# First attention of a fused decoder: heads in pairs, rotation over two banks at once, squared norms streamed

## What is computed

```python
q, k, v = (cproj(Wq), cproj(Wk), cproj(Wv))      # x @ W, real and imaginary halves, (b, n, 16, 64)
qr, kr = q * phase, k * phase                    # phase = cos(ang) + i sin(ang)
s = einsum('bihd,bjhd->bhij', qr, conj(kr)).real
qn = (q.real**2 + q.imag**2).sum(-1)             # kn likewise
E = exp(clip(-mu * |t_i - t_j|, -30, 0))
maha = maximum(qn_i + E*E*kn_j - 2*E*s, 0) / V
logits = coef * log1p(maha / nu) - 0.5*64*log(V), causal
A = softmax(logits); out = A @ v; y = concat(out.real, out.imag) @ Wo
x = layernorm(x + y)
```

## Time and profile before

| | us |
|---|---|
| median of three runs | 3004.72 |
| the runs | 2991.95, 3010.06, 3004.72 |
| span of the profiled execution | 3006.1 |
| TensorE busy in it | 2483.3 (83%) |
| VectorE busy in it | 1809.2 (60%) |

### The profile page before, as it was taken

One profiled execution on the slowest core, in us unless ns is written; L12 is line 12 of the kernel. 1 busy time (PEld: TensorE's weight loads), 2 busy tenths in 40 slices (PEclk: granted clock), 3 DMA queues, 4 the chain that ended last, 5 costly groups with the idle time before them and its releaser, 6 DMA issues.

```text
span 3006.1 us, 41680 instructions
## 1 busy us (share of the span) xinstructions
PE 2483.3 (83%) x14384; PEld 1904.4 (63%) x14384; DVE 1809.2 (60%) x4049; ACT 1131.3 (38%) x2706; POOL 873.9 (29%) x765
## 2 busy tenths in 40 slices
PE   3978979697987979788896979879797888969688
PEld 2666757566675757667575666757576675756544
DVE  8964469524975359634786259653596348852554
ACT  2443325333452325433353324523253333433233
POOL 1531235202541135302452025411353024520100
PEclk8888969797887978889787978879698887879799
DMA  4000000000000000000000000000000000010000
GB/s 152 1 1 1 1 22 1 1 1 22 1 1 1 1 23 1 1 1 1 22 1 1 1 23 1 1 1 1 22 1 1 1 8 15 1 63 1 8 14 14
DMA packets 17083, 32.64 MB, mean 11 GB/s; under 512 B 2686, under 2 KB 8710, under 8 KB 16086
## 3 DMA queue, kind: packets, MB, share of 16 engines
q1 hardware_dynamic: 15574, 25.53, 2.5%
q0 software_dynamic: 1280, 4.20, 0.4%
HBM read 23.43 MB, written 5.77 MB: 10 GB/s over the span
## 4 chain that ended last, share of the span: by engine, by line
PE 54%; DVE 29%; issue 9%; ACT 6%; POOL 1%; DVEq 0%; ACTq 0%; SPq 0%; DMA 0%; POOLq 0%
PE bank L841 50%; DVE work L374 6%; PE bank L845 4%; ACT work L630 4%; DVE work L392 4%; DVE work L383 3%; DVE work L372 2%; DVE st L325 2%; DVE act_row L332 1%; ACT act_T L630 1%; DVE negmax L394 1%; DVE mv L328 1%; ACT ln_t L630 1%; DVE work L528 1%; DVE negmax L525 1%
## 5 line engine op out<-in xcount | busy, mean ns | idle before, releaser
L630 ACT ACTIVATE work<-work 128x512 f32<-128x512 f32 (+1 forms) x584 | 352.2, 624 | 524.1 <-DVE work L528 155.3
L841 PEld LDWEIGHTS bank<-work 128*128 128x128 f32 x3104 | 402.5, 198 | 124.4 <-issue 115.6
L841 PE MATMUL bank<-work 128*128 128x128 f32 x3104 | 429.2, 284 | 40.4 <-DMA work<-in_wo 34.8
L630 ACT ACTIVATE work<-bank 128x512 f32<-128x512 f32 x440 | 250.2, 588 | 312.1 <-PE bank L841 237.3
L374 DVE TENSOR_TENSOR work<-bank,table_space 64x512 f32<-64x512 f32 x512 | 352.3, 688 | 6.8
L823 POOL TENSOR_TENSOR work<-work,sb_cols 128x512 f32<-128x512 f32 x128 | 132.3, 1039 | 742.1 <-ACT work L630 615.9
L841 PE MATMUL bank<-sb_cols,work 128*128 128x1 f32 x2048 | 277.7, 265 | 71.8 <-ACT work L630 71.8
L841 PEld LDWEIGHTS bank<-sb_cols,work 128*128 128x128 f32 x2048 | 275.3, 216 | 91.6 <-ACT work L630 91.6
L630 ACT ACTIVATE work<-bank,sb_b_up 128x512 f32<-128x512 f32 x288 | 197.9, 687 | 270.1 <-PE bank L841 264.8
L841 PEld LDWEIGHTS bank<-sb_w_down,work 128*128 128x128 f32 x2304 | 267.3, 192 | 30.6 <-issue 30.6
L512 DVE SCALAR_TENSOR_TENSOR work<-bank,wexp,work 128x128 f32<-128x128 f32 x256 | 72.1, 344 | 353.9 <-PE bank L841 353.9
(11 more groups left out here) (224 smaller groups left out, 3729.7 us busy)
## 6 DMA issues: line engine op xcount, KB each, us to landing
sb_w_up<-in_w_up SPq DMA_DIRECT2D x1, 2304.0 KB
sb_w_down<-in_w_down SPq DMA_DIRECT2D x1, 2304.0 KB
x_T<-in_x_T POOLq DMA_DIRECT2D x8, 256.0 KB, 2.9
x_row<-in_x_row POOLq DMA_DIRECT2D x8, 256.0 KB, 3.0
ctx_T<-in_ctx_T SPq DMA_DIRECT2D x8, 256.0 KB, 2.9
work<-in_ctx_row SPq DMA_DIRECT2D x8, 256.0 KB, 3.6
out<-act_row SPq DMA_DIRECT2D x8, 256.0 KB, 2.3
x_scratch<-act_row SPq DMA_DIRECT2D x7, 256.0 KB, 2.5
```

The lines of the kernel that those rows point to most:

```text
L630: return nc.scalar.activation(o, i, f, **k)
L841: return nc.tensor.matmul(o, l, r, start=start, stop=stop, skip_group_check=True)
```

## The change

Heads are taken by twos. Step `s` now makes the q (even `s`) or the k (odd `s`) of the pair `p = s // 2`: real parts of both heads in one bank, imaginary parts in the next, the two banks being one tensor `pair_bank` of 128x1024. VectorE multiplies all of it by cosine in one instruction, and by a signed sine with the banks crossed in a second one. GpSimd adds 128x1024 at once. ScalarE squares straight out of `pair_bank`. The norms of a pair are made by a 128x32 selector as the stationary side and the squares as the moving side (`norm_rows_of`, 8 products on 256 columns, each into its own 32 partitions), copied, and turned by two transposes (`norm_cols_of`). The scores of a pair (`scores_of(p)`, steps `s = 2p + 3`) are 16 products of 64 rows instead of 8 of 128, alternating between the row halves of the two heads, into banks 4 and 5. Exponential and scaling work in place in four tiles `M0`. The angle, cosine and sine tables are half as long (8 pairs in place of 16 heads). Pipeline distances grow: distance (`maha`) at step h + 4, logits at h + 5, exponential at h + 6, values and transposes at h + 7, and there are 24 steps in place of 23.

The diff, cut to its added lines and their context (the lines that they replace stand in the functions above; "..." marks what is left out):

```diff
+        pair_bank = ctx.enter_context(nc.psum_tensor("pair_bank", [128, 2, W], fp32))
+        bank = ([pair_bank[:, 0], pair_bank[:, 1]]
+                + [ctx.enter_context(nc.psum_tensor(f"bank{i}", [128, W], fp32)) for i in range(2, 8)])
...
+        table_space = sb("table_space", 128, 4 * H0 * N + 3 * HP * N)
+        dec, dec_inv, wgt, bias_t = (
+            table_space[:, i * H0 * N:(i + 1) * H0 * N].rearrange("p (h n) -> p h n", h=H0) for i in range(4))
+        at = 4 * H0 * N
+        cosT = table_space[:, at:at + HP * N].rearrange("p (h n) -> p h n", h=HP)
+        sin2 = table_space[:, at + HP * N:at + 3 * HP * N].rearrange("p (s h n) -> p s h n", s=2, h=HP)
...
+        by_cos, by_sin = two(0), two(2)
+        q_rot, k_rot = [two(4), two(6)], [two(8), two(10)]
+        sq = [two(12), two(14)]
+        M0 = [wk[16 + i] for i in range(4)]
+        diag = [wk[20], wk[21]]
+        norm_row = wk[22][:, 0:2 * N]
+        attn_space = sb("attn_space", 128, 5, W)
+        v_head = [attn_space[:, i] for i in range(3)]
+        prob_head = [attn_space[:, 3 + i] for i in range(2)]
...
+            for h in range(HP):
                 last = v.tensor_scalar(ang[:, h], tramp[:]
...
+                for s in range(H0 + 8):
+                    if s < H0:
+                        p = s // 2
+                        dve.wait_ge(proj, g * H0 + s + 1)
+                        if s > 0:
+                            dve.wait_ge(rot, g * H0 + s)
+                        R_I = pair_bank[:].rearrange("p r (b n) -> p (r b) n", b=GB)
+                        v.tensor_tensor(by_cos.rearrange("p r (b n) -> p (r b) n", b=GB), R_I,
+                                        cosT[:, p].unsqueeze(1).broadcast_to([128, 2 * GB, N]), ALU.mult)
+                        v.tensor_tensor(by_sin.rearrange("p r (b n) -> p r b n", b=GB),
+                                        pair_bank[:, ::-1].rearrange("p r (b n) -> p r b n", b=GB),
+                                        sin2[:, :, p].unsqueeze(2).broadcast_to([128, 2, GB, N]),
+                                        ALU.mult).then_inc(parts, 1)
+                    h = s - 6
                     if 0 <= h < H0:
                         dve.wait_ge(exped, g * H0 + h + 1)
                         if h >= 2:
                             dve.wait_ge(prob, g * H0 + h - 1)
                         v.reciprocal(rsum[:, h % 2, :], esum[:, h % 4, :]).then_inc(sums_inv, 1)
+                    h = s - 4
                     if 0 <= h < H0:
+                        p, c = h // 2, h % 2
+                        M = rows(M0[h % 4])
+                        dve.wait_ge(norms_sb, g * HP + p + 1)
+                        dve.wait_ge(score, g * HP + p + 1)
+                        if h >= 4:
+                            dve.wait_ge(prob_T, g * H0 + h - 3)
                         for b in range(GB):
+                            last = v.scalar_tensor_tensor(M[:, b], dec_inv[:, h], nrm[:, p % 2, c, b // 2, b % 2:b % 2 + 1],
+                                                          rows(bank[4 + c])[:, b], ALU.mult, ALU.add)
                         link(last)
                         v.scalar_tensor_tensor(M, M, 0.0, bc_h(wgt, h), ALU.min, ALU.mult).then_inc(maha, 1)
+                    h = s - 5
                     if 0 <= h < H0:
+                        M = rows(M0[h % 4])
                         dve.wait_ge(log_done, g * H0 + h + 1)
+                        if h >= 2:
+                            dve.wait_ge(exped, g * H0 + h - 1)
+                        link(v.scalar_tensor_tensor(M, M, coef[:, h:h + 1], bc_h(bias_t, h), ALU.mult, ALU.add))
+                        v.tensor_reduce(negmax[:, h % 2, :], M, X, ALU.max, negate=True).then_inc(logits, 1)
...
+                for s in range(H0 + 8):
+                    h = s - 6
                     if 0 <= h < H0:
                         act.wait_ge(logits, g * H0 + h + 1)
+                        M = rows(M0[h % 4])
                         for b in range(GB):
+                            last = fn(M[:, b], M[:, b], ACT.Exp, bias=negmax[:, h % 2, b:b + 1],
                                       accum_out=esum[:, h % 4, b:b + 1])
                         last.then_inc(exped, 1)
+                    if s < H0:
+                        act.wait_ge(parts, g * H0 + s + 1)
+                        if s >= 2:
+                            act.wait_ge(norm_rows, g * HP + s // 2)
+                        fn(sq[s % 2], pair_bank[:], ACT.Square).then_inc(squares, 1)
+                    p = s // 2 - 1
+                    if s % 2 == 0 and 0 <= p < HP:
+                        act.wait_ge(norm_rows, g * HP + p + 1)
+                        fn(norm_row, bank[3][:, 0:2 * N], ACT.Copy).then_inc(norm_rows_sb, 1)
+                    h = s - 7
                     if 0 <= h < H0:
                         act.wait_ge(v_proj, g * H0 + h + 1)
                         if h >= 3:
                             act.wait_ge(head_out, g * H0 + h - 2)
+                        fn(v_head[h % 3], bank[2][:], ACT.Copy).then_inc(v_sb, 1)
+                    if s % 2 == 0 and 0 <= p < HP:
+                        act.wait_ge(norm_cols, g * HP + p + 1)
+                        fn(nrm[:, p % 2], bank[3][:, 2 * N:4 * N].rearrange("p (i c w) -> p w c i", i=2, c=4)[:, 0:2],
+                           ACT.Copy).then_inc(norms_sb, 1)
+                    h = s - 7
                     if 0 <= h < H0:
                         act.wait_ge(prob_T, g * H0 + h + 1)
                         if h >= 2:
                             act.wait_ge(head_out, g * H0 + h - 1)
+                        fn(prob_head[h % 2], bank[prob_T_bank(h)][:], ACT.Copy).then_inc(prob_T_sb, 1)
+                    h = s - 4
                     if 0 <= h < H0:
                         act.wait_ge(maha, g * H0 + h + 1)
+                        fn(M0[h % 4], M0[h % 4], ACT.Ln, bias=1.0).then_inc(log_done, 1)
...
+                for s in range(H0 + 6):
                     if s < H0:
+                        p = s // 2
+                        pool.wait_ge(parts, g * H0 + s + 1)
+                        if p >= 2:
+                            pool.wait_ge(score, g * HP + p - 1)
+                        q.tensor_tensor((q_rot, k_rot)[s % 2][p % 2], by_cos, by_sin, ALU.add).then_inc(rot, 1)
+                    h = s - 6
                     if 0 <= h < H0:
                         pool.wait_ge(sums_inv, g * H0 + h + 1)
+                        P = rows(M0[h % 4])
                         q.tensor_tensor(P, P, rsum[:, h % 2, :].unsqueeze(2).broadcast_to([128, GB, N]),
                                         ALU.mult).then_inc(prob, 1)
+                    p = s // 2 - 1
+                    if s % 2 == 0 and 0 <= p < HP:
+                        pool.wait_ge(norms_sb, g * HP + p + 1)
+                        if p >= 1:
+                            pool.wait_ge(score, g * HP + p)
+                        for c in range(2):
+                            k_norm = nrm[:, p % 2, c, 2:4].rearrange("p c i -> p (c i)")
+                            q.tensor_tensor(rows(diag[c]), ident[:].unsqueeze(1).broadcast_to([128, GB, N]),
+                                            k_norm.unsqueeze(2).broadcast_to([128, GB, N]),
+                                            ALU.mult).then_inc(diag_done, 1)
...
+                def scores_of(p, g=g):
+                    pe.wait_ge(diag_done, g * H0 + 2 * p + 2)
+                    pe.wait_ge(rot, g * H0 + 2 * p + 2)
+                    if p >= 1:
+                        pe.wait_ge(maha, g * H0 + 2 * p)
+                    for c in range(2):
+                        mm(bank[4 + c][:], dec[:, 2 * p + c], diag[c][:], stop=False)
                     for b in range(GB):
+                        for r in range(2):
+                            for c in range(2):
+                                rr = slice(c * DH0, c * DH0 + DH0)
+                                last = mm(rows(bank[4 + c])[:, b], rows(q_rot[p % 2][rr, r])[:, b],
+                                          rows(k_rot[p % 2][rr, r])[:, b], start=False)
                     last.then_inc(score, 1)
                 def values_of(h, g=g):
...
                         last = mm(rows(bank[2])[:, b], rows(x_T)[:, b], vo[:, h], start=b == 0)
                     last.then_inc(v_proj, 1)
+                def norm_rows_of(p, g=g):
+                    pe.wait_ge(squares, g * H0 + 2 * p + 2)
+                    if p > 0:
+                        pe.wait_ge(norms_sb, g * HP + p)
+                    for r in range(2):
+                        for c in range(4):
+                            last = mm(bank[3][32 * c:32 * c + 32, 0:2 * N], res["norm_sel"][:],
+                                      sq[c // 2][:, r, (c % 2) * 2 * N:(c % 2) * 2 * N + 2 * N], start=r == 0, stop=r == 1)
+                    last.then_inc(norm_rows, 1)
+                def norm_cols_of(p, g=g):
+                    pe.wait_ge(norm_rows_sb, g * HP + p + 1)
```

(59 more changed lines are left out.)

124 lines of the change are left out of this document (15 added, 109 removed).

## The result

The changed kernel takes 3495.79 us (median of 4 runs, 3493.63 to 3496.92) against 3007.39 us (2991.95 to 3034.48, 4 runs): 1.1621 times the time before, 95% interval 1.1556 to 1.1686. The forecast was 3510 us in a range of 3240 to 3820. The profiled execution spans 3492.0 us, 485.9 more than that of before.

The account below looks back on a forecast made before the run. It took a chain of waits between TensorE and VectorE, plus lost clock, to bound the changed kernel: 221 us a group against 157.3, eight times 510 more, 9 less for tables, so 3510 us, range 3240 to 3820.

Parts of the forecast that it names:

- The named wait: TensorE's scores in odd steps wait for VectorE's distance, queued behind this step's projection and rotation: some 5 to 6 us.
- The even step: Projection, rotation, ScalarE's square and copy of the norm rows, then six transposes, one after another: 6.70 us.
- The odd one: Step with the scores: TensorE goes on at 7.56 us, then 7.63 us of its own work, 15.2 in all.
- The meeting that I had counted: VectorE's distance instruction meets GpSimd's addition in odd steps, so TensorE goes on at 7.56 us, 6.5 without it.
- Rival (a): Half-height products in scores and norms don't overlap: 211 us more, 3720; chance 0.28 for this, rival (e) or both.
- rival (e): VectorE's rotation stays at 4.2 us because crossed banks read slower: 3740 us; chance 0.28 for this, Rival (a) or both.
- The clock: TensorE's pauses bring one stretch of low clock a pair, costing 4.4 us: 26.3 us a pair.
- the steps 2 to 5: Early steps of a group's attention: 18.5 us for steps 2 and 3, 24 for steps 4 and 5.
- Rival (b): TensorE's clock holds through the pauses: 187 us a group, 3230 in all; chance 0.16, whole or in part.
- Rival (c): TensorE's clock stays low throughout, 7.5 us more a pair: 3900 us; chance 0.09.
- The tail: End of a group's attention from step 16: distance and logits with waits 27 us, plus 3 for the clock: 30.
- Rival (d): The scores' wait has passed when TensorE arrives; its own work sets 13.7 us a pair: 2915 us; chance 0.04.

Follow-up runs that it names:

- that one block moves: Changed kernel with VectorE's distance of head s - 4 written ahead of the rotation of step s: 3135.64 us, 360 less than the change.
- the addition after the distance: Changed kernel with GpSimd's addition of the rotated halves waiting until the distance of head s - 4 is done: 3465.97 us.
- the filled wait: Changed kernel with seven products nobody reads put into TensorE's wait for the distance in odd steps 5 to 15: 3403.92 us.
- the best order: Changed kernel with distance written first, norm products in the even step, and GpSimd's 1024-column addition split into two of 512: 2920.55 us, 0.9712 of before.

## Why the prediction was right

**The chain of waits: right, and shown.** The named wait is in the trace at its place (6.47 us, ended by L413), and 360 of the 488 us go when that one block moves. The even step was put at 6.70 us and takes 6.55. The odd one was put at 7.56 us to the scores and takes 8.35: VectorE was not free at 974.2 but at 975.09, because in the even step too L413 met GpSimd (1.85 us), which I had counted in the odd step only, and L420 met it as well (1.52 us for 0.74), which I had counted nowhere. The meeting that I had counted was shown by the addition after the distance: 0.69 us.

**TensorE's pieces: scores right, norms half the figure.** Scores 1.99 us for 1.78 (3.56 if the halves didn't overlap). Norms 1.0 us for 1.9: I let neighbours overlap by one pass, and four quarters overlap fully. Rival (a) has fallen. A rotation product takes 1.22 us (1223 ns in the mean of 128), the addition of 1024 columns 2.35 for 2.4: rival (e) has fallen.

**The clock: right in kind, half in size.** I took 4.4 us a pair; it is 2.05 in the pair shown, and 2.2 in the mean of the five (122.1 us against five times the 22.2 of the filled wait at the full clock). The low stretch is 6.8 us, as the shorter of the earlier trace rows, but 2.5 us of it fall into the pause. A pair so takes 24.25 us instead of 26.3, the steps 2 to 5 take 34.6 instead of 42.5. One such stretch a pair, as I took it, holds for the last three pairs only; the first two have 17.0 and 10.2 us of low clock, much of it in pauses. Rival (b) has fallen. Rival (c) has too, since the clock comes back in every pair, but not for the reason that I gave against it: it came back after 17.0 us in one pair, not within 10.2.

**The tail: too small.** I put it at 30 us; it is 40.6 (1037.99 to 1078.6). TensorE's timeline at its start shows the term:

```profile
1037.99 1.16 PE L868 MATMUL bank<-vo,x_T 128*128 128x128 f32 x8
...
1048.60 3.75 PE L868 MATMUL bank<-work,table_space 128*128 128x512 f32 x4 [7.66 <-DVE work L413]
1052.28 2.43 PE L868 MATMUL bank<-work 64*128 64x128 f32 x32
```

The last pair's scores start 10.6 us into the tail, after 7.66 us of waiting for a distance that stands behind exponential and reciprocal, and then run at the low clock; I had let the distances follow at 3.4 us a step without that.

So the forecast of 221 us for a group met 213.5 by pieces that miss in both directions: 9.4 us too much in the five full pairs, 8 too much in steps 2 to 5, 10.6 too little in the tail. In the slower groups, 217.2 to 217.6 us, the total is nearer still; steps 2 to 5 take some 38 us there (in the next group from 1287.22 to 1325.29). The total is nearer than the terms deserve: that part of it is luck. Rival (d), 2915 us, was the price of the design without the chain: the best order measured 2920.55, with a pair at 13.95 us for 13.7. That the two totals are so near is not shown to be more than chance, since the other parts of the group were not compared.

## What to carry to other kernels

Before costing any instruction of a software pipeline, write down for each wait in which step of the other engine its producer stands, and what stands ahead of it there; a consumer in step s whose producer is in step s behind that step's own input makes a chain of both engines, whatever the busy shares say. What lets such a wait bind here is that a pair fills both of banks 4 and 5, which before alternated between heads, so that the next pair has nowhere to go; that further banks would cure it was not tried. Moving the producer forward cost nothing here. A pause of 6 us costs a second time through the clock, and with the clock low a shortened wait may gain little until the pause is gone (30 us, and 68 with the pause filled).

## What the runs showed of the hardware

Products in 32-column quarters run four abreast: 16 passes of 256 columns in 1.02 us, one after another in the same quarter 0.214 us each. Products on alternating 64-row halves take 62 ns a pass (1.99 us for 32) in place of 107 (3.42). Alternating every four passes in place of every two costs 0.09 us of that (2.08); sixteen in a row on one half lose all of it.

A VectorE instruction with two inputs in SBUF (L413) stands still beside the GpSimd addition that began ahead of it, and takes 1.85 us for 0.69. The Trainium skill, "SBUF — State Buffer", Who interferes with whom, says that the later of the two blocks fully until the other is done; the runs agree (0.69 us as soon as the addition starts later, and when the distance is first, the addition is the one that takes longer, 2.96 us in two halves for 2.49), and splitting the GpSimd instruction in two gave 50 us here.

A low clock of TensorE can also follow a short pause: with the long pause filled, a pause of 2.07 us in the even step was the longest one ahead of a stretch of 3.4 us at 1.2 GHz, in two pairs of that run.
